# Four attention-and-expert layers on one core: x loaded in four pieces, one set of normalized tiles, routing in two halves, and the first row's q and k ahead of the routing

## What is computed

```
xn = layernorm(x)
x  = x + attention_l(xn) + experts_l(xn)        for l = 0, 1, 2, 3
```

## Time and profile before

| | |
|---|---|
| three timed runs | 2119.34, 2115.21, 2113.86 us |
| the profiled execution | 2109.61 us, its span 2107.8 us |
| busy in the span | PE 1658.5 us, DVE 1242.1, ACT 772.9, POOL 381.8 |
| mean granted clock of PE | 0.863 |
| phase a and routing of layer 0 | about 29 to 84 us |
| of layer 1 | about 712 to 757 us |
| of layer 2 | about 1125 to 1167 us |
| phase a of layer 3 | about 1655 to 1671 us |

### The profile page before, as it was taken

The page is one execution under the profiler, slowest core; times in us unless marked ns, Lnnn a source line. Parts: engine busy times, 40 slices in busy tenths (PEclk is TensorE's granted clock), DMA queues, the critical chain, the costliest instruction groups (busy, mean ns, idle before and its releaser), DMA issues.

```text
span 2107.8 us, 44050 instructions
## 1 busy us (share of the span) xinstructions
PE 1658.5 (79%) x12743; PEld 1058.8 (50%) x12743; DVE 1242.1 (59%) x3512; ACT 772.9 (37%) x1723; POOL 381.8 (18%) x488
## 2 busy tenths in 40 slices
PE   3276799999766769899886388888883598888888
PEld 3122466766322558778776135555541245454544
DVE  6544455556665476556656356666662666666664
ACT  2022344444322423223222045555551224444444
POOL 1264210101444111111112600000015200000000
PEclk9866799999877778889886579999995679999999
DMA  7021465665211000000000223333321011111110
GB/s 229 29 71 43 132 205 178 188 192 156 57 44 48 0 1 1 0 0 0 0 1 1 72 81 114 119 122 115 110 85 34 18 36 42 44 43 42 40 44 14
DMA packets 133291, 145.07 MB, mean 69 GB/s; under 512 B 15001, under 2 KB 114130, under 8 KB 132946
## 3 DMA queue, kind: packets, MB, share of 16 engines
q1 hardware_dynamic: 100946, 106.20, 16.5%
q10 hardware_dynamic: 26112, 25.17, 4.0%
q0 software_dynamic: 6144, 12.60, 2.0%
HBM read 104.65 MB, written 39.52 MB: 68 GB/s over the span
## 4 chain that ended last, share of the span: by engine, by line
PE 52%; DVE 22%; issue 13%; another core or an unknown queue 4%; DMA 3%; ACT 2%; DVEq 1%; POOL 1%; SPq 1%; ACTq 0%; POOLq 0%
PE pO L706 7%; PE pH L594 5%; PE pT_ L567 5%; PE pY L602 5%; DVE X L1303 4%; PE pH L504 4%; DVE mx L1264 3%; PE pS L653 3%; PE pS L675 3%; DVE stk L1270 2%; PE pT_ L494 2%; PE pT_ L565 2%; PE pY L516 2%; PE pT_ L556 1%
## 5 line engine op out<-in xcount | busy, mean ns | idle before, releaser
L816 ACT ACTIVATE pex<-pT_ 128x512 f32<-128x512 f32 (+1 forms) x768 | 427.8, 562 | 665.0 <-PE pT_ L567 260.3
L1264 DVE TENSOR_REDUCE mx<-pS 128x2 f32<-128x512 f32 x512 | 346.6, 688 | 212.4 <-PE pS L544 86.6
L567 PE MATMUL pT_<-stk 32*128 32x256 f16 x1024 | 205.5, 290 | 83.1 <-DVE mx L1264 46.2
L544 PE MATMUL pS<-stk 32*128 32x256 f16 x1024 | 215.5, 299 | 34.3 <-DMA stk<-packed_qk 19.2
L706 PE MATMUL pO<-pex,va 128*9 128x256 f32 (+1 forms) x3072 | 206.9, 391 | 2.0 <-ACT pex L816 2.0
L809 ACT ACTIVATE wb<-pH,b 128x256 f32<-128x256 f32 x256 | 107.3, 470 | 271.0 <-PE pH L504 271.0
L906 POOL TENSOR_TENSOR qk<-qkf,qk 128x512 f16<-128x512 f32 x48 | 55.5, 1156 | 732.5 <-DVE qk L1240 367.0
L567 PEld LDWEIGHTS pT_<-stk 32*128 32x128 f16 x1024 | 55.6, 94 | 212.3 <-DVE mx L1264 94.3
L504 PE MATMUL pH<-XT,w 128*128 (+1 forms) x512 | 146.1, 412 | 0.0
L819 ACT ACTIVATE xts<-pO 128x256 f32<-128x256 f32 x192 | 73.9, 385 | 175.2 <-PE pO L706 126.1
L594 PE MATMUL pH<-xsT,wb 128*128 128x128 f32 x888 | 131.4, 293 | 1.8 <-ACT hbs L787 1.8
(11 more groups left out here) (197 smaller groups left out, 2903.2 us busy)
## 6 DMA issues: line engine op xcount, KB each, us to landing
wb<-in_w SPq DMA_DIRECT2D x111, 514.0 KB, 3.8
stk<-packed_qk ACTq DMA_DIRECT2D x96, 256.0 KB, 2.6
packed_qk<-qk SPq DMA_DIRECT2D x144, 128.0 KB, 1.9
xsb<-sorted_x SPq DMA_DIRECT2D x111, 64.0 KB, 3.4
sorted_y<-ysb SPq DMA_DIRECT2D x111, 64.0 KB, 3.1
sorted_x<-wb SPq DMA_DIRECT2D x3, 1536.0 KB, 12.5
w<-in_w SPq DMA_DIRECT2D x2, 1024.0 KB
out<-X SPq DMA_DIRECT2D x16, 128.0 KB, 1.8
```

The lines of the kernel that those rows point to most:

```text
L544: return pe.matmul(bank[:, part * T:(part + 1) * T], stk[rows, side, j, part * P:(part + 1) * P], stk[rows, side, j, T:2 * T], start=True, ...
L567: return pe.matmul(bank[:, part * T:(part + 1) * T], key, stk[rows, side, j, 0:T], start=True, stop=True)
L816: act.activation(pex[:, k % 8, 0:n], bank[:, 0:n], ACT.Exp).then_inc(s("T_free"), 1)
L1264: ins = dve.tensor_reduce(mx[:, :, j, col], bank.rearrange("p (c n) -> p c n", c=2), AX.X, ALU.max)
```

## The change

It has five parts.

1. x is loaded in four pieces with a semaphore each; SP raises only the shared semaphores ahead of them, the others behind. DVE waits for a piece before its first tile.
2. In all four layers DVE writes each normalized tile once, into `XN`, and PE turns it from there. ACT makes one copy, to `XT`, from which the logits are formed too. The loop is written out, with the logits of group g - 1 behind the turning of group g.
3. `choose`, the part of the routing up to the chosen experts, works on 16 tiles at a time. The first half is called in front of the turns, when four of eight groups of logits are there. ACT issues the two exponentials at g = 7 and g = 8 of its phase a.
4. In layers 0 and 2 the second half, `places` and the counting on PE come behind turn -2, that is behind the first row's P. POOL waits for the places only at the end of its turn -2.
5. `start_search` comes behind the rise of "gates".

Cut to its core:

```diff
 def run_turns(eng, layer, body, unlooped=0, behind_first=None):
     for n in range(-2, loop_from):
         body(Turn(layer, n))
+        if n == -2 and behind_first is not None:
+            behind_first()
...
-            "ld_x": [(X[:, 0:16, :], xin[:, 0:16, :]), (X[:, 16:32, :], xin[:, 16:32, :])],
+            **{f"ld_x{c}": [(X[:, 8 * c:8 * c + 8, :], xin[:, 8 * c:8 * c + 8, :])] for c in range(4)},
...
+                def turned(g):
+                    pe.wait_ge(sem("xn_ready"), PRIMED + l * (NT // 4) + g + 1)
+                    pe.wait_ge(sem("xts_ready"), PRIMED + l * (NT // 4) + g - 1)
+                    for u in range(4):
+                        ins = pe.transpose(pS[:, g % 2, u * P:(u + 1) * P], XN[:, 4 * g + u, :], ident[:, :])
+                    ins.then_inc(sem("turned"), 1)
+                def logits(g):
+                    pe.wait_ge(sem("xts_ready"), PRIMED + l * (NT // 4) + g + 1)
+                    pe.wait_ge(sem("logits_copied"), PRIMED + min(l, 3) * (NT // 4) + g - 1)
...
+                for g in range(NT // 4 + 1):
+                    if g < NT // 4:
+                        turned(g)
+                    if l < 3 and g > 0:
+                        logits(g - 1)
...
-                if l < 3:
+                if l == 1:
                     pe.wait_ge(sem("gates"), PRIMED + l + 1)
+                def rank_tokens():
+                    pe.wait_ge(sem("chosen"), 1 + SORTED.index(l))
+                    pe.wait_ge(sem(f"L{l}_S_free"), PRIMED + ring_uses(l, "S", -2))
...
+                    pe.wait_ge(sem("gates"), PRIMED + l + 1)
+                run_turns(pe, l, take_turn, behind_first=rank_tokens if l in SORTED else None)
...
+            def exponents(l, part):
+                half = slice(NT // 2 * part, NT // 2 * (part + 1))
+                act.wait_ge(sem("shifted"), PRIMED + 2 * l + part + 1)
+                act.activation(pr[:, half, 0:EXPERTS[l]], ra[:, half, 0:EXPERTS[l]], ACT.Exp)\
+                   .then_inc(sem("exp_logits"), 1)
+                for g in range(NT // 4 + 1):
+                    if g < NT // 4:
+                        act.wait_ge(sem("turned"), PRIMED + l * (NT // 4) + g + 1)
+                        act.activation(XT[:, g * 4 * P:(g + 1) * 4 * P], pS[:, g % 2, :], ACT.Copy)\
                            .then_inc(sem("xts_ready"), 1)
+                    if l < 3 and g > 0:
+                        act.wait_ge(sem("logits"), PRIMED + l * (NT // 4) + g)
+                        act.activation(LG[:, (g - 1) * 4:g * 4, 0:EXPERTS[l]],
...
+                    if l < 3 and g >= NT // 4 - 1:
+                        exponents(l, g - NT // 4 + 1)
...
-                    if turn.n == -2:
+                    if turn.n == -2 and l in SORTED:
+                        if l == 0:
+                            pool.wait_ge(sem("places_zeroed"), 16 * -(-MAXBLOCKS // ZEROED_BLOCKS))
+                        pool.wait_ge(sem("places_ready"), 1 + SORTED.index(l))
                         scatter(sorts)
...
+                for g in range(NT // 4):
+                    dve.wait_ge(sem("rstd"), PRIMED + l * (NT // 4) + g + 1)
+                    for t in range(4 * g, 4 * g + 4):
+                        ins = dve.tensor_scalar(XN[:, t, :], X[:, t, :], MV[:, t, 0:1], rstd[:, t:t + 1],
+                                                ALU.subtract, ALU.mult)
+                    ins.then_inc(sem("xn_ready"), 1)
+            def choose(l, part):
+                n = EXPERTS[l]
+                half = slice(NT // 2 * part, NT // 2 * (part + 1))
...
+            def routing(l):
+                choose(l, 1)
                 if l == 1:
                     chain.link(dve.memset(GA[:, :, 15:16], 1.0))
-                if l == 0:
-                    start_search()
                 if l in SORTED:
                     places(l)
                 dve.sem_inc(sem("gates"), 1)
+                if l == 0:
+                    start_search()
...
                 if l < 3:
+                    dve.wait_ge(sem(f"ld_{l}"), full[f"ld_{l}"])
+                    choose(l, 0)
+                if l == 1:
                     routing(l)
...
-                run_turns(dve, l, lambda turn: take_turn(turn, tc))
+                run_turns(dve, l, lambda turn: take_turn(turn, tc),
+                          behind_first=(lambda: routing(l)) if l in SORTED else None)
...
+            for name in shared:
+                sp.sem_inc(sem(name), PRIMED)
+            load_inputs(of_x)
             for name in primed:
-                sp.sem_inc(sem(name), PRIMED)
+                if name not in shared:
+                    sp.sem_inc(sem(name), PRIMED)
+            load_inputs([group for group in loads if group not in of_x])
```

More of the change, by code:

```diff
@@ L209, in use, with run_turns @@
         return self.loop * (2 * ring_uses(self.layer, ring, self.n)) + before
-def run_turns(eng, layer, body, unlooped=0):
+def run_turns(eng, layer, body, unlooped=0, behind_first=None):
     last = B if layer == 1 else B + 1
@@ L478, in phase_a @@
             def phase_a(l):
[L480 to L496 removed]
+                def turned(g):
[7 more added lines that the diff above has]
+                    pe.wait_ge(sem("logits_copied"), PRIMED + min(l, 3) * (NT // 4) + g - 1)
+                    for u in range(4):
+                        t = 4 * g + u
+                        ins = pe.matmul(pT_[:, g % 2, u * 16:u * 16 + EXPERTS[l]], XT[:, t * P:(t + 1) * P],
+                                        wr[l][:, :], start=True, stop=True)
+                    ins.then_inc(sem("logits"), 1)
+                for g in range(NT // 4 + 1):
[3 more added lines that the diff above has]
+                        logits(g - 1)
             def hidden(l, turn, k, use, s):
@@ L831, in _ @@
             for l in range(4):
-                if l < 3:
-                    phase_a(l)
-                    act.wait_ge(sem("shifted"), PRIMED + l + 1)
-                    act.activation(pr[:, :, 0:EXPERTS[l]], ra[:, :, 0:EXPERTS[l]], ACT.Exp)\
-                       .then_inc(sem("exp_logits"), 1)
-                else:
-                    phase_a(l)
+                phase_a(l)
                 if l == 1:
@@ L973, in _ @@
             chain.link(dve.memset(gst[:, :, :, :], 0.0))
-            dve.wait_ge(sem("ld_x"), full["ld_x"])
             def phase_a(l):
@@ L997, in routing @@
-            def routing(l):
-                s = lambda n: sem(f"L{l}_{n}")
-                n = EXPERTS[l]
-                full_e = lambda a: a[:, :, None].to_broadcast([P, NT, n])
-                lg, p_, a_, b_, c_, g_, k_ = (x[:, :, 0:n] for x in (LG, pr, ra, rb, rc, GA, rank))
-                dve.wait_ge(sem(f"ld_{l}"), full[f"ld_{l}"])
-                dve.wait_ge(sem("logits_copied"), PRIMED + l * (NT // 4) + NT // 4)
+                for g in range(NT // 4):
[4 more added lines that the diff above has]
+                    ins.then_inc(sem("xn_ready"), 1)
@@ L1005, in routing @@
+            def choose(l, part):
+                n = EXPERTS[l]
+                half = slice(NT // 2 * part, NT // 2 * (part + 1))
+                full_e = lambda a: a[:, half, None].to_broadcast([P, NT // 2, n])
+                lg, p_, a_, b_, c_, g_, k_ = (x[:, half, 0:n] for x in (LG, pr, ra, rb, rc, GA, rank))
+                m1, m2 = r1[:, half], r2[:, half]
+                dve.wait_ge(sem("logits_copied"), PRIMED + l * (NT // 4) + NT // 8 * (part + 1))
                 if l > 0:
-                    chain.link(dve.tensor_tensor(lg, lg, br[l][:, None, :].to_broadcast([P, NT, n]), ALU.add))
@@ L1011, in routing @@
-                chain.link(dve.reciprocal(r2[:, :], r1[:, :]))
+                dve.wait_ge(sem("exp_logits"), PRIMED + 2 * l + part + 1)
+                chain.link(dve.tensor_reduce(m1, p_, AX.X, ALU.add))
+                chain.link(dve.reciprocal(m2, m1))
                 chain.link(dve.tensor_tensor(p_, p_, full_e(r2), ALU.mult))
                 for k in range(TOPK[l]):
-                    chain.link(dve.tensor_reduce(r1[:, :], p_, AX.X, ALU.max))
+                    chain.link(dve.tensor_reduce(m1, p_, AX.X, ALU.max))
@@ L1171, in combine @@
                 for t in tiles:
+                    if t < NT and not gathered and t % 8 == 0:
+                        dve.wait_ge(sem(f"ld_x{t // 8}"), 16)
                     if t < NT and gathered:
@@ L1452, in sp_turn, with load_inputs @@
                         load(l, k, k)
+            def load_inputs(groups):
+                for group in groups:
+                    for dst, src in loads[group]:
+                        sp.dma_start(dst, src).then_inc(sem(group), 16)
+            of_x = [group for group in loads if group.startswith("ld_x")]
+            shared = [name for name in primed if name in SHARED_SIGNALS]
+            for name in shared:
+                sp.sem_inc(sem(name), PRIMED)
+            load_inputs(of_x)
             for name in primed:
-                sp.sem_inc(sem(name), PRIMED)
```

(6 more changed lines are left out.)

79 lines of the change are left out of this document (12 added, 67 removed).

## The result

The changed kernel takes **2065.97 us** (median of four runs, 2065.83 to 2069.75), the kernel before beside it 2116.26 us. The ratio is 0.9766, 95% interval 0.9748 to 0.9783. Two later sessions, on two chips, gave 0.9737 (0.9683 to 0.9791) and 0.9790 (0.9750 to 0.9829). The gain of the medians was 50.3, 49.5 and 44.3 us. The forecast was 26 us with a range down to 2077 us: the sign was right, the size was not.

A forecast was written before the change was run, and what follows sets the result against it. The prediction took the layer starts, where engines wait for one another in single file, as the bound. Terms -19.2 + 1.2 - 3.5 - 4.5 = -26.0 us on the profiled execution gave 2089 us for timed runs, range 2077 to 2101.

The forecast's parts named there:

- The length of phase a: Layers 0 to 2: PE turns and forms logits without gaps, 22.25 us together from summed row times.
- The load: Start of layer 0: x lands earlier, so statistics and all behind them move 7.8 us, from 18.01 to 10.14.
- Layer 3: Start of layer 3: DVE's eight groups of 1.17 us set the pace; -4.5 us, bounds -5 and -4.
- the rival of the risen clock: Gapless phase a of layers 0 to 2: PE's clock rises, total -46 us, 2069 us; chance 0.08.
- The halves: Routing in two halves: half-width steps save only 0.14 or 0.26 us each, so only a little is hidden.
- trap: First half of choose waits until PE has nearly ended, its exponential standing behind ACT's copy of the seventh group's logits.
- Layer 1's +1.2: Layer 1: two half-width chains cost more than PE's shorter phase gives, +1.2 us, bounds 0 and +2.5.
- The blocked DVE: Layer 0: DVE waits beside POOL's split, 1.5 of 3.0 us; rival: blocked for all of it, 2091 us, chance 0.13.
- P ahead and the search: Layer 0: P hidden before the second half, search (2.36 us) behind "gates"; first scatter at 72.3 against 93.01.
- POOL's shift: Layer 2: row values wait for POOL behind 16 scatters, so the first scatter's shift counts, -3.5 us, bounds -10 and -2.
- a rival on the slower side: Layers 0 and 2: early head steps beside scatters wait 2.8 us more each, +11 us, 2126 us; chance 0.03.
- a give-back: Layer 0, turns 0 to 2: scatters and spread-DMA waits shift against each other, losing 12 us, 2101 us; chance 0.16.

The follow-up runs named there:

- group 3: Four kernels beside the kernel before (2000.56 us) on one chip: changed kernel paced 1965.93, kernel before paced 2001.25, paced with P behind routing 1976.92, spread further 1943.97 us.
- the turnings first: Changed kernel with all 32 tiles turned before any logits are formed in phase a of layers 1 and 2: 2072.88 us.
- phase a alone: Kernel before with only part 2 (tiles normalized once, one copy, gapless phase a): 2078.81 us, ratio 0.9906.
- paced changed kernel: Changed kernel with scatters and gathers of turns 0 to 2 and 11 to 16 held to one per head step: 2014.23 us (0.9585); on another chip 1965.93 us (0.9813).

## Why the prediction was right or wrong

Two steps of the sum failed. The length of phase a was taken too long: 22.25 us for 20.1, with layer 3 2.2 us short besides, 9 us of the gain together. And the turns between the starts were put at nothing, where the medians leave 9 to 15 us more; what brings those is open. With phase a and layer 3 at their measured size the forecast would have been 35 us, 2080 us, and the measured time would still lie 14 us below it.

**The load: right.** Statistics at 10.17 (10.2 forecast); undoing it moved the first scatter by 7.55 (7.8).

**Phase a: the step that failed, in its size.** I summed 22.25 us out of 0.975 us for a turning and 1.79 for the logits. In the gapless phase a group takes 2.45 us, because in the rows the logits begin before the turning ends (26.39 against 25.50 + 1.09) and the next turning before the logits end (27.96 against 26.39 + 1.72), and it lasts 20.1 us to the last logits. That is 2.2 us in each of three layers: -21.4 for -19.2, -1.0 for +1.2, and most of -6.0 for -3.5. Row times of instructions that overlap may be added only as distances from start to start.

**Layer 3: right in kind, 2.2 us short.** DVE's eight groups took 8.3 us instead of 9.36, and the clock rose. That was the rival of the risen clock, in the one layer where I had not put it; in layers 0 to 2 PE ran no faster and it did not come true. Where the clock did not rise in layer 3 either and POOL's `rstd` set the pace, in group 3, the stretch gave 3.6 us, less than my bound of 4. The Trainium skill, "TensorE: Matmul & The Clock Gate", section "What's actually happening", makes the clock follow how busy PE has been. Busy by the profile's rows does not decide alone here. Turnings without a gap rose (layer 3, and layer 1 with the turnings first), turnings 0.2 us apart stayed at 0.50 (layer 3 in group 3, layer 2 with the turnings first), and so did 20 us of turnings and logits without a gap.

**The halves: right, trap and all.** DVE sat 6.84 us on the exponential, and a routing of one piece is as fast. Layer 1's +1.2 was its cost against phase a's gain; unhalved, the layer gained 3.3 us. **The blocked DVE**: 1.8 us of the 3.0 that POOL's split takes, nearer my 1.5 than the full 3.0, whose rival fell.

**P ahead and the search: right** in what POOL's first scatter shows (4.2, 2.2 and 2.36 us).

**POOL's shift or the head steps'.** I argued that POOL's shift counts in layer 2. Without long waits it does: 52.0 and 52.1 us from first scatter to the split of turn 0. With them, that stretch was 5.5 us longer before than after in the first profiles, and 7.9 with P put back. But it was 6.2 longer too with the load undone, where P is ahead, and 0.4 with phase a alone, where P is behind. So that late head steps meet more of them is argued and not shown.

**What was missing: the long waits.** I had seen them, priced them only as a rival on the slower side and as a give-back, and took the turns between for unchanged. They fall by chance and by chip. Where they are absent the change gives 35.3 us, with both kernels paced; where they are there, three comparisons gave 44 to 50. Where the 9 to 15 us more lie is open: from execution to execution of one kernel layer 0's turns alone differ by 8 us, only one profile of the kernel before has the waits, and their sum hardly differs (93 us before, 81, 95 and 90 in the three profiles of the changed kernel). Some of it is none of these waits: from its first split on, layer 3 has none, and yet was 3.2, 3.1 and 1.6 us shorter in the three profiles of the changed kernel, for a reason that is open. Which mechanism holds the two engines up is open too. That it takes POOL's indirect DMAs is shown for turns 0 to 2 of layer 0, where the waits went with them; that these are not enough is shown by group 3.

**Layer 1's turns** took 4.5 us more in the first profile and 367.9 to 376.8 us in others. The kernel before lies within that spread, so this can't be laid to the change. The granted clock sags once in most turns there.

## What to carry to other kernels

Split a measured gain into stretches that move alike in every execution and turns that don't, and profile the same kernel twice before reading a shift in the latter. Halving a chain hides its first half only if every engine it calls on has its instruction early enough in its own order; look for the in-order neighbour. Indirect DMAs issued back to back can go with long waits of engines that have nothing to do with them: issuing one per head step instead was worth some 30 to 41 us on one chip, nearly as much as the whole studied change, and nothing on another.

## What the hardware showed that I had not expected

- DVE and ACT wait beside POOL's indirect DMAs, mostly 2 to 9 us at a time, on three chips and not on a fourth; in the profiles of unpaced kernels with all their scatters together 71 to 105 us of a span of 2056 to 2108 us, and besides 22 to 27 us in one piece beside the gathers at layer 2's end. The paced changed kernel took 0.9585 of the kernel before on a chip with them, where the change alone gives about 0.977; and pacing, put on the kernel before, gave nothing (0.9989) on the chip without.
- The granted clock rose where PE only turned without a gap (0.50 to 1.00 at 1625.8, and 0.96 from 701 to 704), stayed at 0.50 where turnings stood 0.2 us apart, and fell in gapless logits. The Trainium skill, "TensorE: Matmul & The Clock Gate", section "Part 4: PE-mode transpose", says that the full clock doesn't engage for transpose-mode; these rows show it engaging during `pe.transpose` of float32.
